# An adaLN transformer block on one core: a VectorE chain rewritten with tensor_tensor, its constants and mean handed to ScalarE, and weight splits spread over more key tiles

## The reference, cut to what matters

```
h = layernorm(x) * (1 + ca) + sa
x = x + ga * attention(h)                 # softmax over the query axis
h = layernorm(x) * (1 + cb) + sb
x = x + gb * fp4_ffn(h)

fp4_linear(x, w):  both operands in blocks of 16:
    scale = max(max|block| / 6, 1e-12)
    block -> nearest of {0, .5, 1, 1.5, 2, 3, 4, 6} * sign * scale
fp4_ffn(h) = fp4_linear(silu(fp4_linear(h, w_gate)) * fp4_linear(h, w_up), w_down)
```

## Time and profile before

| | |
|---|---|
| median of 3 runs | 1882.34 us (1882.11 to 1883.11) |
| the profiled execution | 1882.75 us, span of the core 1881.4 us |
| PE, DVE, ACT, POOL busy | 91%, 92%, 76%, 32% of the span |
| mean granted TensorE clock | 0.966 of full speed |
| DMA | 88.51 MB, 47 GB/s on average |
| costliest groups | DVE maximum L1034 1180.8 us, ACT exponential L773 1141.1 us, PE L581 1070.5 us |

### The profile page before, as it was taken

One profiled execution on the slowest core, in us unless ns is written; L12 is line 12 of the kernel. 1 busy time (PEld: TensorE's weight loads), 2 busy tenths in 40 slices (PEclk: granted clock), 3 DMA queues, 4 the chain that ended last, 5 costly groups with the idle time before them and its releaser, 6 DMA issues.

```text
span 1881.4 us, 38310 instructions
## 1 busy us (share of the span) xinstructions
PE 1707.4 (91%) x15378; PEld 843.2 (45%) x15378; DVE 1735.0 (92%) x2028; ACT 1428.3 (76%) x2553; POOL 593.5 (32%) x1018
## 2 busy tenths in 40 slices
PE   6999999999999998999899999999998778878887
PEld 5642223222222235732222222222235777878776
DVE  5789999999999997699799999999997999999985
ACT  4279999999999995399799999999994333333332
POOL 1112222222222221014612221222225766665663
PEclk9999999999999999999999999999999889898988
DMA  5201110111001112201010111011121111121000
GB/s 188 78 1 33 39 44 29 32 39 45 29 31 39 46 58 76 75 31 38 29 41 29 33 39 44 29 33 39 44 95 47 56 65 68 65 68 65 12 9 18
DMA packets 52434, 88.51 MB, mean 47 GB/s; under 512 B 3232, under 2 KB 34848, under 8 KB 52256
## 3 DMA queue, kind: packets, MB, share of 16 engines
q1 hardware_dynamic: 51840, 85.54, 14.0%
q10 hardware_dynamic: 416, 0.53, 0.1%
HBM read 56.69 MB, written 29.36 MB: 46 GB/s over the span
## 4 chain that ended last, share of the span: by engine, by line
PE 40%; ACT 23%; issue 16%; POOL 12%; DVE 8%; POOLq 0%; DVEq 0%; ACTq 0%
PE acc L581 24%; ACT e_sb L773 19%; PE slot L552 7%; PE acc L419 5%; POOL o_lo L887 3%; POOL e_sb L1328 3%; PE slot L419 2%; POOL hqT_lo L887 2%; POOL rstd L1302 2%; DVE nm L1034 1%; ACT e_sb L847 1%; PE acc L616 1%; ACT hqT_hi L697 1%; PE slot L639 1%; DVE e_sb L1132 1%
## 5 line engine op out<-in xcount | busy, mean ns | idle before, releaser
L1034 DVE TENSOR_REDUCE nm<-slot 128x1 f32<-128x1024 f32 x1024 | 1180.8, 1212 | 12.8 <-PE slot L552 12.7
L773 ACT ACTIVATE e_sb<-slot,nm 128x1024 f32<-128x1024 f32 x1024 | 1141.1, 1114 | 33.8 <-DVE nm L1034 32.7
L581 PE MATMUL acc<-e_sb,vp 64*64 64x512 f32 x8192 | 1070.5, 596 | 42.1 <-ACT ost L793 38.6
L552 PE MATMUL slot<-stq,stk 64*64 64x512 f16 x4096 | 418.9, 393 | 14.7 <-ACT e_sb L773 14.7
L552 PEld LDWEIGHTS slot<-stq,stk 64*64 64x64 f16 x4096 | 118.7, 104 | 673.8 <-ACT e_sb L773 634.8
L581 PEld LDWEIGHTS acc<-e_sb,vp 64*64 64x64 f32 x8192 | 284.2, 133 | 200.5 <-issue 95.7
L1280 POOL TENSOR_TENSOR dlt<-nm 128x4 f32<-128x4 f32 x128 | 25.7, 201 | 688.1 <-DVE nm L1034 688.1
L773 ACT ACTIVATION_READ_ACCUMULATOR e_sb<-slot,nm 128x1 f32 x1024 | 197.3, 193 | 0.0
L837 ACT COPY xqT<-acc 128x256 f32<-128x256 f32 x32 | 11.9, 373 | 171.6 <-PE acc L616 171.6
L1271 POOL TENSOR_TENSOR vp<-v_sb,fac 128x512 f32<-128x512 f32 x128 | 134.5, 1051 | 10.0
L1254 POOL TENSOR_TENSOR wsum<-cor,ssum 128x8 f32<-128x8 f32 x128 | 26.0, 203 | 265.1 <-ACT cor L801 265.1
(11 more groups left out here) (191 smaller groups left out, 2159.1 us busy)
## 6 DMA issues: line engine op xcount, KB each, us to landing
stk<-qk_parts SPq DMA_DIRECT2D x128, 128.0 KB
o_heads<-ost SPq DMA_DIRECT2D x64, 256.0 KB, 3.5
v_sb<-o_heads SPq DMA_DIRECT2D x8, 2048.0 KB, 8.1
...
stq<-qk_parts SPq DMA_DIRECT2D x128, 64.0 KB
...
```

The costliest lines, as they stand in the source:

```text
L552: mm = pe.matmul(slot[s][side * VD:(side + 1) * VD, c * 512:(c + 1) * 512], stk[c * 64:c * 64 + 64, h % 2, i * P + side * VD:i * P + (side ...
L581: mm = pe.matmul(acc[half * VD:(half + 1) * VD, c * 512:(c + 1) * 512], vp[rows, g % 3, gi, half, :], e_v[rows, j % ERING, n0:n0 + 512], s ...
L773: act.activation(e_v[:, j % ERING, half * 1024:(half + 1) * 1024], slot[u % 3][:, :], ACT.Exp, bias=nm[:, g % 4, i, half:half + 1], accum_ ...
L1034: dve.tensor_reduce(nm[:, g % 4, i, half:half + 1], slot[u % 3][:, :], AX.X, ALU.max, negate=True).then_inc(maxed.sem)
```

## The change

- In the token tiles all scalar_tensor_tensor instructions of VectorE become tensor_tensor. The factor 1/6 (`sixth`), the factor just below one (`below`) and the epsilon are tensors in SBUF; each factor is an instruction of its own on the block scales (60 wide).
- `mix_normalise` multiplies the 704 and the 256 columns in two instructions, each with an event of its own; `square` on ScalarE is in two parts too, and is followed by an Identity over all 960 columns that adds FLOOR and writes `mix_big` in f32, which the two snap instructions of VectorE then use.
- The layer norm's subtraction of the mean and multiplication by rstd go to ScalarE (`stretch`, writing `zx`), between `split_heads` and `silu`. GpSimd makes -mean * rstd for it (`nmean`, `shift`) in `inverse_root2`. VectorE is left with the product with `cb1` and the sum with `sbr`.
- The fold and the split of the output projection of GpSimd take one instruction in each of the key tiles 24 to 71 (`split_wo`), instead of one in 16 and four in 8 key tiles.
- `fold_wd(0, ...)` moves from the end of attention to after `scale_mix(2)`, `fold_wd(1, ...)` and `split_down(0)` each one step later; `low_heads(2)` goes between the first two inverse roots; `wgu_lo` is made in two parts, one behind each of the steps 0 and 1.

```diff
@@ scalar engine, end of attention
                         high(wgu_hi[k][:, :], wguT[:, k, :]).then_inc(wgu_high.sem)
+                    split_heads(2)
+                    stretch(0)
                     square(1)
-                    split_heads(2)
+                    stretch(1)
@@ def square(i)
-            act.wait_ge(*mix_normal.past(i - 1))
-            act.activation(mix_sq[:, lo:hi], mix_n[:, lo:hi], ACT.Square, scale=SQUARE).then_inc(mix_squared.sem)
+            if lo == 0:
+                act.wait_ge(*hid_normal.past(i - 3))
+                ins = act.activation(mix_sq[:, 0:F], mix_n[:, 0:F], ACT.Square, scale=SQUARE)
+            if hi > F:
+                act.wait_ge(*in_normal.past(i - 1))
+                ins = act.activation(mix_sq[:, F:hi], mix_n[:, F:hi], ACT.Square, scale=SQUARE)
+            ins.then_inc(mix_squared.sem)
+            act.wait_ge(*mix_squared.past(i - 1))
+            if i >= 2:
+                act.wait_ge(*mix_snapped.past(i - 2))
+            act.activation(mix_big[:, lo:hi], mix_sq[:, lo:hi], ACT.Identity, bias=floor[:, 0:1]).then_inc(mix_floored.sem)
+
+        def stretch(i):
+            act.wait_ge(*rstd2_made.past(i))
+            if i:
+                act.wait_ge(*stretched.past(i - 1))
+            act.activation(zx, x2_r[:, i % 7, :], ACT.Identity, bias=shift[:, i % 2:i % 2 + 1],
+                           scale=rstd[:, i % 2, 0:1]).then_inc(zx_made.sem)
@@ vector engine, end of attention
-                    dve.wait_ge(*wgu_high.past(1))
-                    low(dve, wgu_lo[:, 0, :], wguT[:, 0, :], wgu_hi[0][:, :])
-                    low(dve, wgu_lo[:, 1, :], wguT[:, 1, :], wgu_hi[1][:, :]).then_inc(wgu_low.sem)
                     dve.wait_ge(*attended.past(B * JT - 5))
                     for i in range(2):
                         ffn_step(i)
+                        dve.wait_ge(*wgu_high.past(i))
+                        low(dve, wgu_lo[:, i, :], wguT[:, i, :], wgu_hi[i][:, :]).then_inc(wgu_low.sem)
@@ def token_input(i)
-            dve.scalar_tensor_tensor(mix[:, F:F + D], x2_r[:, i % 7, :], mv[:, i % 2, 0, 0:1], cb1[:, i // NT, :],
-                                     ALU.subtract, ALU.mult).then_inc(centred.sem)
-            dve.wait_ge(*centred.past(i))
-            dve.wait_ge(*rstd2_made.past(i))
-            dve.scalar_tensor_tensor(mix[:, F:F + D], mix[:, F:F + D], rstd[:, i % 2, 0:1], sbr[:, i // NT, :],
-                                     ALU.mult, ALU.add).then_inc(input_made.sem)
+            dve.wait_ge(*zx_made.past(i))
+            dve.tensor_tensor(mix[:, F:F + D], zx, cb1[:, i // NT, :], ALU.mult).then_inc(stretched.sem)
+            dve.wait_ge(*stretched.past(i))
+            dve.tensor_tensor(mix[:, F:F + D], mix[:, F:F + D], sbr[:, i // NT, :], ALU.add).then_inc(input_made.sem)
@@ def mix_normalise(i)
+            settle(dve.tensor_tensor(amax, amax, sixth[:, b0:b1], ALU.mult))
-            settle(dve.scalar_tensor_tensor(scale, amax, 1.0 / 6.0, tiny[:, b0:b1], ALU.mult, ALU.max))
+            settle(dve.tensor_tensor(scale, amax, tiny[:, b0:b1], ALU.max))
             settle(dve.reciprocal(inv, scale))
-            dve.scalar_tensor_tensor(blocks(mix_n[:, lo:hi]), blocks(mix[:, lo:hi]), BELOW_ONE, wide(inv, nb),
-                                     ALU.mult, ALU.mult).then_inc(mix_normal.sem)
+            settle(dve.tensor_tensor(inv, inv, below[:, b0:b1], ALU.mult))
+            if lo == 0:
+                dve.tensor_tensor(blocks(mix_n[:, 0:F]), blocks(mix[:, 0:F]), wide(qs[:, 2, 0:44], 44),
+                                  ALU.mult).then_inc(hid_normal.sem)
+            if hi > F:
+                dve.tensor_tensor(blocks(mix_n[:, F:hi]), blocks(mix[:, F:hi]), wide(qs[:, 2, 44:60], 16),
+                                  ALU.mult).then_inc(in_normal.sem)
@@ def mix_snap(i)
-            dve.scalar_tensor_tensor(mix_n[:, lo:hi], mix_sq[:, lo:hi], FLOOR, mix_n[:, lo:hi],
-                                     ALU.add, ALU.add).then_inc(mix_added.sem)
+            dve.tensor_tensor(mix_n[:, lo:hi], mix_n[:, lo:hi], mix_big[:, lo:hi], ALU.add).then_inc(mix_added.sem)
             dve.wait_ge(*mix_added.past(i - 1))
-            dve.scalar_tensor_tensor(mix_n[:, lo:hi], mix_sq[:, lo:hi], FLOOR, mix_n[:, lo:hi],
-                                     ALU.add, ALU.subtract, reverse1=True).then_inc(mix_snapped.sem)
+            dve.tensor_tensor(mix_n[:, lo:hi], mix_n[:, lo:hi], mix_big[:, lo:hi], ALU.subtract).then_inc(mix_snapped.sem)
@@ def split_wo(c, s), in place of cut_wo(c)
+            if s == 0:
+                fold_wo(0, c)
+            elif s == 1:
...
+            else:
+                fold_wo(1, c)
@@ def attend_pool(b)
-                if b == B - 1 and 24 <= j < 48:
-                    n, c = divmod(j - 24, 8)
-                    if n < 2:
-                        fold_wo(n, c)
-                    else:
-                        cut_wo(c)
+                if b == B - 1 and 24 <= j < 72:
+                    split_wo(*divmod(j - 24, 6))
                 if j == JT + 2 and b == B - 1:
                     pool.wait_ge(*vp_made.past(B * JG - 1))
-                    for c in range(FCH):
-                        fold_wd(0, c)
                     inverse_root2(0)
+                    low_heads(2)
                     inverse_root2(1)
                     scale_mix(1)
-                    low_heads(2)
@@ def inverse_root2(i)
             pool.wait_ge(*var2_made.past(i))
-            pool.tensor_tensor(rstd[:, i % 2, 0:1], ve[:, i % 2, 0:1], mhalf[:, 0:1], ALU.pow).then_inc(rstd2_made.sem)
+            if i >= 2:
+                pool.wait_ge(*zx_made.past(i - 2))
+            pool.tensor_tensor(nmean[:, i % 2:i % 2 + 1], zero[:, 0:1], mv[:, i % 2, 0, 0:1], ALU.subtract)
+            sem, n = pool_own.next()
+            pool.tensor_tensor(rstd[:, i % 2, 0:1], ve[:, i % 2, 0:1], mhalf[:, 0:1], ALU.pow).then_inc(sem)
+            pool.wait_ge(sem, n)
+            pool.tensor_tensor(shift[:, i % 2:i % 2 + 1], nmean[:, i % 2:i % 2 + 1], rstd[:, i % 2, 0:1],
+                               ALU.mult).then_inc(rstd2_made.sem)
```

More of the change, by code:

```diff
@@ L150, in adaln_block @@
         tiny = sb("tiny", [P, 60])
-        zero = sb("zero", [P, 1])
+        sixth = sb("sixth", [P, 60])
+        below = sb("below", [P, 60])
+        constants = sb("constants", [P, 3])
+        epsilon, zero, floor = constants[:, 0:1], constants[:, 1:2], constants[:, 2:3]
+        shifts = sb("shifts", [P, 4])
+        nmean, shift = shifts[:, 0:2], shifts[:, 2:4]
         cut = sb("cut", [P, D])
@@ L222, in adaln_block @@
         mix_q = region(e_sb, 4192, 2, F + D)
+        mix_big = region(v_sb, 14592, F + D)
+        zx = region(e_sb, 6112, D)
         sg = region(e_sb, 7136, 2, F)
@@ L874, in scalar_program @@
                     split_heads(i + 1)
+                if i < TILES:
+                    stretch(i)
                 if i <= TILES + 1:
                     silu(i - 2)
-                if i == 2:
+                if i == 3:
                     split_down_act(0)
@@ L1091, in token_variance @@
             dve.wait_ge(*moments.past(2 * i + 1))
[L1092 to L1093 removed]
+            dve.tensor_tensor(ve[:, i % 2, 0:1], mv[:, i % 2, 0, 1:2], epsilon[:, 0:1], ALU.add).then_inc(var2_made.sem)
         def token_input(i):
[L1096 to L1101 removed]
+            dve.wait_ge(*zx_made.past(i))
+            dve.tensor_tensor(mix[:, F:F + D], zx, cb1[:, i // NT, :], ALU.mult).then_inc(stretched.sem)
+            dve.wait_ge(*stretched.past(i))
+            dve.tensor_tensor(mix[:, F:F + D], mix[:, F:F + D], sbr[:, i // NT, :], ALU.add).then_inc(input_made.sem)
         def hidden_product(i):
@@ L1213, in fold_wo, with split_wo @@
             pool.tensor_tensor(wob[b][:, c, :], wo_s[:, c, :], ga[:, b, :], ALU.mult).then_inc(wo_folded.sem)
-        def cut_wo(c):
-            sem, n = pool_own.next()
-            pool.wait_ge(*wo_folded.past(c))
-            pool.tensor_scalar(cut[:, :], wob[0][:, c, :], SPLITTER, None, ALU.mult).then_inc(sem)
-            pool.wait_ge(sem, n)
-            sem, n = pool_own.next()
-            pool.tensor_tensor(wob_cut[:, c, :], cut[:, :], wob[0][:, c, :], ALU.subtract).then_inc(sem)
-            pool.wait_ge(sem, n)
-            pool.tensor_tensor(wob_hi[0][:, c, :], cut[:, :], wob_cut[:, c, :], ALU.subtract).then_inc(wo_cut.sem)
-            pool.wait_ge(*wo_cut.past(c))
-            low(pool, wob_lo[0][:, c, :], wob[0][:, c, :], wob_hi[0][:, c, :]).then_inc(wo_low.sem)
+        def split_wo(c, s):
+            if s == 0:
+                fold_wo(0, c)
+            elif s == 1:
+                pool.wait_ge(*wo_folded.past(2 * c))
+                pool.tensor_scalar(cut[:, :], wob[0][:, c, :], SPLITTER, None, ALU.mult).then_inc(wo_times.sem)
+            elif s == 2:
+                pool.wait_ge(*wo_times.past(c))
+                pool.tensor_tensor(wob_cut[:, c, :], cut[:, :], wob[0][:, c, :], ALU.subtract).then_inc(wo_rest.sem)
```

(19 more changed lines are left out.)

15 lines of the change are left out of this document (6 added, 9 removed).

## The result

The changed kernel takes 1937.7 us (median of 4 runs, 1937.25 to 1941.8) against 1882.22 for the kernel before (4 runs, 1881.32 to 1883.11): a ratio of 1.030, 95% interval 1.0282 to 1.0317. The forecast was 1952.0 with a range of 1912 to 1985.

What follows compares the result with a forecast made beforehand. The bound was taken to be a loop of VectorE and GpSimd instructions waiting for each other at the SBUF port, with ScalarE between. 1882.3 - 12.2 + 1 + 76.9 + 4 = 1952.0 us, range 1912 to 1985.

Steps and rivals of the forecast that it cites:

- The spread: Attention: one GpSimd cut in each of 48 key tiles no longer delays the differences; -12.2 us, bounds -13 and -10.
- (a): Token tile, normalise: both input operations wait for the scaling, hqT_lo holds the second small operation; +0.9 us, bounds 0.3 and 1.2.
- (b): Token tile, ScalarE from the 704 part to o_hi: two Squares and the Identity; +1.3 us, bounds 1.1 and 1.5.
- (c): Token tile, o_lo: it starts later against the VectorE instruction ahead, so waits less; -0.25 us, bounds -0.3 and 0.
- (d): Token tile, o_lo's end to the scaling: snap subtract, mean subtract, power and nmean product in a row; +0.7 us, bounds 0.2 and 1.0.
- Sum of a tile: Token tile: the four loop terms together, +2.65 us, so 16.2 us a tile; +76.9 us over 29 tiles.
- Entry: Between attention and the tile loop: up to 3 us gained, moved folds and wd split against it; +1 us, bounds -3 and +6.
- drain: Steps 32 and 33, without stretch: longer ScalarE and small operations remain; +4 us, bounds 2 and 6.
- Doesn't take the port: Rival, token tile: tensor_tensor escapes the wait, so input operations run under the scaling; -0.8 us a tile, 1847 us; chance 0.06.
- Only the count matters: Rival, token tile: VectorE's added operations cost some 0.75 us a tile, waits cover ScalarE's detour; 1892 us; chance 0.07.
- TensorE the bound: Rival, token tile: longer idle lowers TensorE's clock to a mean of 0.55, 18.2 us a tile; 2009 us; chance 0.03.

Runs made afterwards that it cites:

- e7: Changed kernel with every tensor_tensor of the chain written as scalar_tensor_tensor with a factor of 1.0: 1938.03 us, ratio 1.0297.
- e3: Changed kernel without the stretch, mean and rstd applied by VectorE again: 1908.25 us, ratio 1.0139.
- e1: Kernel before with only the output projection's fold and split spread over key tiles 24 to 71: 1868.09 us, ratio 0.9931.
- e6: Changed kernel with eight more matmuls a tile behind `down`, read by nobody, to keep TensorE at work: 1938.46 us, ratio 1.03.
- e2: e1 plus the new normalise alone: three 60-wide operations instead of one, the 960-wide product as one tensor_tensor: 1878.06 us, ratio 0.9983.
- e4: Changed kernel without ScalarE's Identity: one Square of 960 columns, snap as scalar_tensor_tensor with FLOOR in it: 1920.8 us, ratio 1.0207.
- e5: Changed kernel with GpSimd's o_lo made for 256 of 1024 columns, the projection reading the high part instead: 1887.7 us, one run.

## Why the prediction was right, and where its sizes were off

The sign, the size and the mechanism came out, the places in the loop only in part; 14.3 us of the 69.7 forecast are missing in the medians (1952.0 against 1937.7).

- **tensor_tensor waits at the port like scalar_tensor_tensor.** Shown by the timelines of the changed kernel and by e7. By the Trainium skill (SBUF — State Buffer, Who interferes with whom) the instruction that issues first holds the port to its end; the traces agree in both directions, hqT_lo ahead of `below` in the changed kernel, and the 704 part 0.01 us ahead of hqT_lo in e3.
- **The spread, -12.2.** -12.05 in the profiles, -13.3 in the medians of e1. Right.
- **One tile for all.** The prediction took 13.58 us and the order of one tile for the whole stage, and six of 26 tiles had the other order. Averaged over the 26 tiles the terms are +1.19 (a, to the end of the 704 part), +1.23 (b), -0.21 (c) and +0.17 (d), where 0.9, 1.3, -0.25 and 0.7 were forecast: (a) is too low by about 0.3, (d) too high by about 0.5, and that they partly cancel is luck. The readings below are of the tiles that are shown.
- **(a) Normalise, +0.9.** The sum of the tile's first half is right, its place is not. Forecast was that the second small operation would be held and the 704 part end 1.85 to 1.9 us after hqT_lo. It was the third, and the end 1.00 after, as before; but TensorE, idle for 4.29 us, turned at the lower level of its clock, and hqT_lo itself came 0.89 us later. Forcing the clock up (e6) brings the forecast picture, `tiny` held and 1.82 us, for the same time. Alone in the old kernel (e2) the edit costs 0.34 a tile, as a mean of two kinds of tile. The rest of the term needs the input pair to be late, which is the stretch's doing: from the scaling's end to o_hi's start are on average 6.35 us in the kernel before, 8.12 in e3 and 8.77 in the changed kernel. Of the 2.42 (b) has 1.23 and the stretch 0.65; 0.54 are left for the new normalise.
- **(b) ScalarE to o_hi, +1.3.** 2.18 us against 0.95: +1.23. The Identity took 1.10 us, as worked out from the pointer operands. Undone, it gives 0.84 at that place and 0.67 a tile (e4).
- **(c) o_lo, -0.25.** 2.39 us to its successor's start against 2.70: -0.31. Right.
- **(d) o_lo's end to the scaling, +0.7.** This term failed in size: from the start of o_lo's successor to the scaling 1.82 us against 1.42, so +0.40. I had put the held instruction's 1.02, a power of 0.68, a gap and 0.20 in a row. The negation (L1332) did end behind L1163 (1.10), but the power took 0.54 and the product overlaps its successor, 0.14 from start to start. In this tile (d) is the one term that was too high by more than 0.1. Of the 14.3 us missing, the 27 tiles of the table have 6.9 (71.6 forecast, 64.7 measured).
- **Sum of a tile, +2.65.** Measured +2.21 in this tile and 64.7 / 27 = +2.40 on the average.
- **Entry +1 and drain +4.** The entry and the term of tile 3 came to +1.65 where 3.65 stood, the end with one tile to +2.4 where 6.6 stood. Both were taken somewhat too high; no experiment parted them.
- **Rivals.** "Doesn't take the port" is refuted by e7 and the timelines. "Only the count matters" would have given 1885 for e2 and 1892 for the whole; both times rule it out, though in half of e2's tiles the small operations cost what it says. By the Trainium skill (VectorE: DVE Perf Modes, Rules for kernel authors) one minimises the number of chained operations; the direction fits this case, but e5 shows the price elsewhere, since 1.65 us of one VectorE instruction went away with no VectorE work removed. "TensorE the bound" is refuted by e6, where more matmuls cost nothing.

The parts undone one by one don't add up: e2 puts 10.0 us on the normalise, e4 gives back 16.9, e3 29.5, together 56.4 of the 69.6 us between e1 and the changed kernel. Entry and drain are in the rest; how much of it is interplay at the lock was not measured. Each edit moves the moment at which the next pair of instructions meets at the port, so an edit's price depends on the others.
